# Local attention layers of a gated model on one core: key turn, key scaling, maxima and Gelu moved within their slot

## Chip, cores and metric

The kernel runs on one core of one Trainium2 chip. The metric is the device time of one execution in microseconds.

## The reference, cut to what matters

A residual stream x (4 batches, 256 tokens, 128 features) goes through four gated pairs of a cross attention and a feed-forward block. The change touches one of these eight blocks, `_L0_ffn`, which is itself a stack of six layers of windowed attention with a feed-forward behind each:

```
for i in range(DEPTH):                       # 6
    x = attn_layer(shift_tokens(x), Wqkv[i], q_scale[i], k_scale[i], Wo[i]) + x
    x = ffn_layer(shift_tokens(x), ln_g[i], ln_b[i], W1[i], b1[i], W2[i], b2[i]) + x
```

`attn_layer` has 16 heads of 64. Queries and keys are divided by their norm, scaled and rotated (q * cos + rotate_half(q) * sin). Each token looks at the 32 tokens of its own window and the 32 before, with a mask; then a softmax, the weighted values and the output projection. `ffn_layer` is a layer norm, a projection to 2 x 341, `a * gelu(gate)` and a projection back.

## The kernel before, in words

Everything is float32. The five engines run one program each and meet in semaphores. After a first cross attention (to about 178 us) the local layers run to about 978 us; the other blocks follow in a part called the drain. The change is in the local layers alone.

Their work is cut into 96 units (6 layers x 4 batches x 2 halves of the tokens x 2 halves of the heads, `unit_of`). One unit is 128 tokens x 8 heads x 64. The loops run over 96 slots. In slot s each engine does one step of several units: the projections of unit s, the turns (transposes) of unit s - 2, scores of s - 3, softmax sums of s - 4, weighted values of s - 5, the output of s - 6. The constants TURN, SCORE, SOFT, VALUE, OUT are these lags. Four units make one batch of a layer, and the feed-forward of that batch is spread over later slots by further lags (CENTRE 10 to RENEW 15); `ended(slot, lag)` is true in one slot of four. So slots come in rounds of four. I name a slot by s mod 4: in kind 0 are the gate projections (L663, L672 on TensorE, L1952 on ScalarE), in kind 1 is Gelu (L1966, L1967, a table load before and behind it) with the hidden projections L680 to L689, in kind 2 the centring L256, its variance L266 and the output projection L698 of the feed-forward; kind 3 has none of them on TensorE. The order within a slot is the order of the calls in `pe_local`, `act_local`, `dve_local` and `pool_local`, written by hand. SyncE (`sync_program`) only moves weights and the value windows.

The steps, in the order of a slot, with the line of each:

- TensorE: query projection L722, turn of queries L751, output projection L823, value L742 and key projection L731, turn of the softmax weights L792, scores L781 (64 small matmuls), weighted values L808 (64 small matmuls), turn of keys L759. Turned queries and turned keys share one PSUM bank, so L751 waits for the key copy (`k_kept`) and L759 for the query copy (`q_kept`). L698 and L689 wait for the mask (`masked`) of their slot, since the scores' bank holds their result.
- ScalarE: square of queries L1876, exponential L1921, copies out of PSUM of turned queries L1897, values L1890, square of keys L1883, copy of turned weights L1928, copy of turned keys L1906, copy of the weighted values L1936, then the norms L1912, L1914, L1916 (1/|q| and 1/|k| of the unit, from the sums of squares).
- VectorE: residual L2902, L2903; products with cos and sin for queries and for keys (L2861 to L2863, twice), between them the softmax sum L2891; the mask L2883, maxima L2885; the hidden product L2918 (waits for Gelu); the sums of squares L2870 and L2871.
- GpSimd: division by the softmax sum L4004, sum of the key products L3978, scaling of queries by their norm L3985, sum of the query products L3973, subtraction of the maxima L3998, scaling of keys L3992. In the last slot of a layer it makes the rotary tables of the next (L644).

Of the kernel before, what the change touches and what calls it, by code (L numbers as in the profile page):

```python
# [707 lines left out]
def live(u):  # L708
    return 0 <= u < UNITS
# [126 lines left out]
def pe_local(e, s, m):  # L836
    for slot in range(LOCAL_SLOTS):
        if live(slot):
            pe_query(e, s, m, slot)
        if live(slot - TURN):  # L840
            pe_turn_query(e, s, m, slot - TURN)
        if live(slot - OUT):
            pe_out(e, s, m, slot - OUT)
        if ended(slot, GATES) is not None:
            pe_gates(e, s, m, ended(slot, GATES))
        if live(slot):
            pe_value(e, s, m, slot)
            pe_key(e, s, m, slot)
        if slot == 0:
            e.wait_ge(s["x_done"], B)  # L850
            pe_ln_centre(e, s, m, m.bank[FB], m.x[B - 1])
        if slot == 1:
            pe_ln_var(e, s, m, 2 * B - 1, ln_views(m.ln_local), m.bank[FB])
        if ended(slot, CENTRE) is not None:
            pe_centre(e, s, m, ended(slot, CENTRE))
        if live(slot - VALUE):
            pe_turn_weights(e, s, m, slot - VALUE)
        if live(slot - SCORE):
            pe_scores(e, s, m, slot - SCORE)
        if live(slot - VALUE):  # L860
            pe_weighted(e, s, m, slot - VALUE)
        if ended(slot, VAR) is not None:
            pe_var(e, s, m, ended(slot, VAR))
        if ended(slot, OPEN) is not None:
            pe_hidden(e, s, m, ended(slot, OPEN))
        if ended(slot, LAST) is not None:
            pe_last_hidden(e, s, m, ended(slot, LAST), min(slot - SCORE + 1, UNITS))
        if ended(slot, GATE2) is not None:
            pe_last_gate(e, s, m, ended(slot, GATE2))
        if live(slot - TURN):  # L870
            pe_turn_key(e, s, m, slot - TURN)
        if ended(slot, MERGE) is not None:
            pe_ffn_out(e, s, m, ended(slot, MERGE), min(slot - SCORE + 1, UNITS))

# [1096 lines left out]
def act_local(e, s, m):  # L1971
    for slot in range(LOCAL_SLOTS):
# [18 lines left out]
            act_gates(e, s, m, ended(slot, KEEP))  # L1991
        if ended(slot, SQUARE) is not None:
            act_ln_start(e, s, m, ended(slot, SQUARE))
        if ended(slot, GELU) is not None:
            act_gelu(e, s, m, ended(slot, GELU))
        if live(slot - TURN):
            act_key(e, s, m, slot - TURN)
        if live(slot - VALUE):
            act_out(e, s, m, slot - VALUE)
        if live(slot) and slot >= RAMP:  # L2000
            act_norm(e, s, m, slot)
        if slot == 0:
# [871 lines left out]
def dve_mask(e, s, m, u):  # L2874
# [6 lines left out]
    if u >= ES:  # L2881
        e.wait_ge(s["p_turned"], u - ES + 1)
    e.tensor_tensor(p.rearrange("p (z r k) -> p z r k", z=2, r=UP), scores, band, ALU.add).then_inc(s["masked"], 1)  # L2883
    e.wait_ge(s["masked"], u + 1)
    e.tensor_reduce(m.local_small[u % 4][:, 16:24], split(p, UH), AX.X, ALU.max).then_inc(s["most"], 1)  # L2885


def dve_total(e, s, m, u, link):
# [57 lines left out]
def dve_local(e, s, m, link):  # L2946
    for slot in range(LOCAL_SLOTS):
# [13 lines left out]
            dve_products(e, s, m, slot, 1)  # L2961
        if live(slot - SCORE):
            dve_mask(e, s, m, slot - SCORE)
        if ended(slot, MIX) is not None:
            dve_hidden(e, s, m, ended(slot, MIX))
        if live(slot):
            dve_norm(e, s, m, slot)
        if slot == 2:
            dve_first_z(e, s, m, B - 1, m.bank[FB], ln_views(m.ln_local)[1])

# [1042 lines left out]
def pool_local(e, s, m):  # L4013
    for slot in range(LOCAL_SLOTS):
# [8 lines left out]
            pool_add_query(e, s, m, slot)  # L4023
        if live(slot - 1) and slot <= RAMP:
            pool_norm_key(e, s, m, slot - 1)
        if live(slot - SCORE):
            pool_lower(e, s, m, slot - SCORE)
        if live(slot - 1) and slot > RAMP:
            pool_norm_key(e, s, m, slot - 1)
        if live(slot):  # L4030
            stage = unit_of(slot)[1]
            if slot % (B * LAYER_UNITS) == B * LAYER_UNITS - 1 and stage < DEPTH:
# [570 lines left out]
```

## Time and profile before

| | |
|---|---|
| median of 3 runs | 1283.91 us (1281.17 to 1284.33) |
| span of the profiled execution | 1280.5 us |
| that execution's own time | not given apart from its span |
| TensorE busy | 1215.7 us (95%) |
| VectorE busy | 986.7 us (77%) |
| ScalarE busy | 938.3 us (73%) |
| GpSimd busy | 785.7 us (61%) |
| mean granted TensorE clock | 0.988 of full |

Busy time counts an instruction from start to end; matmuls are pipelined, so a new one starts before the one in front of it ends, and 95% doesn't say that TensorE is at its peak. How far one group of matmuls starts behind another is the better measure of its pace. The span is from the first instruction to the last.

### The profile page before, as it was taken

What the parts mean: (1) busy time and instruction counts of PE and PEld (TensorE: products, weight loads), DVE (VectorE), ACT (ScalarE), POOL (GpSimd) and SP (SyncE); (2) the same over time, 40 slices, a digit from 0 to 9 for tenths busy, and PEclk for the clock granted to TensorE, in tenths of its full rate; (3) what the DMA queues carried; (4) which work ended last, traced back from release to release, by engine and by line L of the source; (5) the groups of instructions that cost most, each with busy time, mean ns of one, the idle gap of its engine ahead of it and who ended that gap; (6) DMA issues with size and microseconds to landing.
All of it is one profiled execution on the core that took longest, in us unless ns stands there. A gap on an engine that the chain in (4) does not pass through costs nothing.

```text
span 1280.5 us, 44796 instructions
## 1 busy us (share of the span) xinstructions
PE 1215.7 (95%) x17900; PEld 871.3 (68%) x17900; DVE 986.7 (77%) x2513; ACT 938.3 (73%) x2310; POOL 785.7 (61%) x805
## 2 busy tenths in 40 slices
PE   7999988999999999999999999999999999999996
PEld 5777745676767667767777677767677877777553
DVE  4666677888888788888888888888888656778677
ACT  6777775677777677777777777777777758788891
POOL 3444447878878787788777877778776102635000
PEclk9999998999999999999999999999999989999989
DMA  5000032222224322342225222422232001202000
GB/s 213 1 2 1 2 116 73 70 61 58 61 62 110 96 60 63 82 127 57 63 59 149 58 63 64 128 79 61 62 86 54 2 15 74 83 32 92 1 1 17
DMA packets 71743, 81.89 MB, mean 64 GB/s; under 512 B 15456, under 2 KB 63584, under 8 KB 71024
## 3 DMA queue, kind: packets, MB, share of 16 engines
q1 hardware_dynamic: 71536, 79.03, 22.4%
q8 instruction: 143, 2.34, 0.8%
q14 instruction: 64, 0.52, 0.1%
HBM read 31.22 MB, written 0.56 MB: 25 GB/s over the span
## 4 chain that ended last, share of the span: by engine, by line
PE 46%; DVE 19%; ACT 18%; issue 11%; POOL 5%; DMA 1%; SPq 0%; DVEq 0%; ACTq 0%; POOLq 0%
PE banks L823 3%; PE banks L808 3%; PE banks L391 2%; DVE arena L2862 2%; DVE arena L2861 2%; DVE small L2870 2%; PE banks L1143 2%; PE banks L1137 2%; PE banks L420 2%; DVE arena L2883 2%; DVE arena L2863 2%; DVE small L2871 2%; PE banks L1165 2%; PE banks L405 2%; PE banks L751 2%
## 5 line engine op out<-in xcount | busy, mean ns | idle before, releaser
L3998 POOL TENSOR_TENSOR arena<-arena,small 128x512 f32<-128x512 f32 x93 | 97.1, 1044 | 136.2 <-DVE small L2885 136.2
L1906 ACT ACTIVATE arena<-banks 128x512 f32<-128x512 f32 x94 | 56.1, 597 | 139.5 <-PE banks L759 139.3
L2861 DVE TENSOR_TENSOR arena<-banks,rotary 128x512 f32<-128x512 f32 x192 | 131.6, 685 | 22.7 <-ACT arena L1876 9.2
L3973 POOL TENSOR_TENSOR arena<-arena 128x512 f32<-128x512 f32 x96 | 122.7, 1278 | 26.3 <-DVE arena L2863 26.2
L808 PE MATMUL banks<-arena 64*64 64x32 f32 x5824 | 107.3, 221 | 15.5 <-issue 8.3
L3978 POOL TENSOR_TENSOR arena<-arena 128x512 f32<-128x512 f32 x95 | 121.4, 1278 | 0.2 <-DVE arena L2863 0.2
L607 POOL TENSOR_TENSOR arena<-arena,small 128x512 f32<-128x512 f32 x64 | 66.6, 1041 | 89.0 <-DVE small L534 89.0
L808 PEld LDWEIGHTS banks<-arena 64*64 64x64 f32 x5824 | 95.8, 135 | 27.0 <-ACT arena L1928 11.4
L3985 POOL TENSOR_TENSOR arena<-arena,small 128x512 f32<-128x512 f32 x95 | 99.5, 1047 | 5.6 <-ACT small L1916 5.6
L722 PE MATMUL banks<-slot,z 128*128 128x512 f32 x192 | 100.1, 603 | 1.3 <-DVE arena L2863 0.9
L3992 POOL TENSOR_TENSOR arena<-arena,small 128x512 f32<-128x512 f32 x95 | 99.2, 1044 | 0.0
L742 PE MATMUL banks<-slot,z 128*128 128x512 f32 x192 | 98.2, 593 | 0.0
L731 PE MATMUL banks<-slot,z 128*128 128x512 f32 x192 | 98.0, 592 | 0.0
L823 PE MATMUL banks<-arena,slot 128*128 128x128 f32 x720 | 97.9, 279 | 0.0
L4004 POOL TENSOR_TENSOR arena<-arena,small 128x512 f32<-128x512 f32 x91 | 95.0, 1044 | 0.0
L751 PEld LDWEIGHTS banks<-constants,arena 128*128 128x128 f32 x376 | 42.0, 142 | 75.4 <-issue 68.1
L461 ACT ACTIVATE arena<-arena,small 128x256 f32<-128x256 f32 x128 | 63.8, 501 | 39.7 <-DVE small L566 39.7
L823 PEld LDWEIGHTS banks<-arena,slot 128*128 128x128 f32 x720 | 88.0, 192 | 0.5
L2902 DVE TENSOR_TENSOR z<-z,banks 64x128 f32<-64x128 f32 x90 | 25.0, 278 | 75.4 <-PE banks L823 75.4
L781 PE MATMUL banks<-arena 64*32 64x64 f32 x5952 | 81.1, 225 | 0.5 <-issue 0.5
L2863 DVE TENSOR_TENSOR arena<-banks,rotary 128x256 f32<-128x256 f32 x192 | 79.6, 415 | 0.0
L2862 DVE TENSOR_TENSOR arena<-banks,rotary 128x256 f32<-128x256 f32 x192 | 79.6, 414 | 0.0
(403 smaller groups left out, 3368.8 us busy)
## 6 DMA issues: line engine op xcount, KB each, us to landing
arena<-arena SPq DMA_DIRECT2D x576, 64.0 KB, 2.1
slot<-in_pack_dram SPq DMA_DIRECT2D x28, 339.5 KB, 3.4
arena<-arena SPq DMA_DIRECT2D x288, 32.0 KB, 1.9
slot<-in_pack_dram SPq DMA_DIRECT2D x2, 2713.5 KB, 9.2
slot<-in_pack_dram SPq DMA_DIRECT2D x1, 2693.5 KB
slot<-in_pack_dram SPq DMA_DIRECT2D x1, 2316.5 KB
arena<-gate_store SPq DMA_DIRECT2D x8, 256.0 KB, 3.9
slot<-in_pack_dram SPq DMA_DIRECT2D x4, 337.0 KB, 3.6
```

The costliest lines, as they stand in the source:

```text
L722: e.matmul(m.bank[QB], m.zs[b][:, t * P:(t + 1) * P], m.W(stage, "Wqkv")[:, half * BANK:(half + 1) * BANK], start=True, stop=True, skip_gr ...
L731: e.matmul(m.bank[KB], m.zs[b][:, t * P:(t + 1) * P], m.W(stage, "Wqkv")[:, at:at + BANK], start=True, stop=True, skip_group_check=True).t ...
L742: e.matmul(m.bank[VB], m.zs[b][:, t * P:(t + 1) * P], m.W(stage, "Wqkv")[:, at:at + BANK], start=True, stop=True, skip_group_check=True).t ...
L808: made = e.matmul(m.bank[PB if x else VB][y * DH:(y + 1) * DH, to:to + WINDOW], v[rows, i, k, :], pT[rows, at:at + WINDOW], start=True, st ...
L823: made = e.matmul(m.bank[S0][:, N:N + P], wo[:, c * D:(c + 1) * D], oT[:, k * P:(k + 1) * P], start=(k == 0), stop=(k == UP - 1), skip_gro ...
L2861: e.tensor_tensor(rot, made, cos, ALU.mult)
L2862: e.tensor_tensor(sinp[:, :, 0:mid], made[:, :, mid:DH], sin[:, :, 0:mid], ALU.mult)
L2863: e.tensor_tensor(sinp[:, :, mid:DH], made[:, :, 0:mid], sin[:, :, mid:DH], ALU.mult).then_inc(s["k_products"] if k else s["q_products"], 1)
L3973: e.tensor_tensor(m.rot_q[u % ROTS], m.rot_q[u % ROTS], m.sin_q[u % 2], ALU.add).then_inc(s["q_added"], 1)
L3978: e.tensor_tensor(m.rot_k[u % ROTS], m.rot_k[u % ROTS], m.sin_k[u % 2], ALU.add).then_inc(s["k_added"], 1)
L3985: e.tensor_tensor(q, q, stretch(m.local_small[u % 4][:, 0:UH], DH), ALU.mult).then_inc(s["q_rotated"], 1)
L3992: e.tensor_tensor(k, k, stretch(m.local_small[u % 4][:, UH:2 * UH], DH), ALU.mult).then_inc(s["k_rotated"], 1)
```

## The change

Four things are moved within a slot, on all four computing engines, and nothing else is touched.

```diff
 def pe_local
         if live(slot - VALUE):
             pe_turn_weights(e, s, m, slot - VALUE)
+        if live(slot - TURN):
+            pe_turn_key(e, s, m, slot - TURN)
         if live(slot - SCORE):
             pe_scores(e, s, m, slot - SCORE)
...
             pe_last_gate(e, s, m, ended(slot, GATE2))
-        if live(slot - TURN):
-            pe_turn_key(e, s, m, slot - TURN)

 def act_local
-        if ended(slot, GELU) is not None:
-            act_gelu(e, s, m, ended(slot, GELU))
         if live(slot - TURN):
             act_key(e, s, m, slot - TURN)
         if live(slot - VALUE):
             act_out(e, s, m, slot - VALUE)
+        if ended(slot, GELU) is not None:
+            act_gelu(e, s, m, ended(slot, GELU))

     e.tensor_tensor(p.rearrange("p (z r k) -> p z r k", z=2, r=UP), scores, band, ALU.add).then_inc(s["masked"], 1)
+
+
+def dve_most(e, s, m, u):
     e.wait_ge(s["masked"], u + 1)
-    e.tensor_reduce(m.local_small[u % 4][:, 16:24], split(p, UH), AX.X, ALU.max).then_inc(s["most"], 1)
+    e.tensor_reduce(m.local_small[u % 4][:, 16:24], split(m.e[u % ES], UH), AX.X, ALU.max).then_inc(s["most"], 1)

 def dve_local
             dve_mask(e, s, m, slot - SCORE)
+        if live(slot):
+            dve_norm(e, s, m, slot)
+        if live(slot - SCORE):
+            dve_most(e, s, m, slot - SCORE)
         if ended(slot, MIX) is not None:
             dve_hidden(e, s, m, ended(slot, MIX))
-        if live(slot):
-            dve_norm(e, s, m, slot)

 def pool_local
+        if live(slot - 1) and slot > RAMP:
+            pool_norm_key(e, s, m, slot - 1)
         if live(slot - SCORE):
             pool_lower(e, s, m, slot - SCORE)
-        if live(slot - 1) and slot > RAMP:
-            pool_norm_key(e, s, m, slot - 1)
```

TensorE in a slot of kind 1, first before and then changed (L792 turns weights, L759 keys, L751 queries; L781 scores, L808 weighted values):

```order
L792 MATMUL banks<-constants,arena 128x128 [waits o_kept,normalised]
L792 MATMUL banks<-constants,arena 128x128 x3
L781 MATMUL banks<-arena 32x64 [waits a2_done,masked,z_ready,y_added,k_kept]
L781 MATMUL banks<-arena 32x64 x31
L808 MATMUL banks<-arena 64x32 [waits v_kept,v64_even,p_kept]
L808 MATMUL banks<-arena 64x32 x31
L680 MATMUL banks<-xn,slot 128x256 [waits gate2_kept]
L681 MATMUL banks<-xn,slot 128x256
L689 MATMUL banks<-xn,slot 85x256 [waits masked]
L759 MATMUL banks<-constants,arena 128x128 [waits q_kept,k_rotated]
L759 MATMUL banks<-constants,arena 128x128 x3
L722 MATMUL banks<-slot,z 128x512 [waits q_products]
```

```order
L792 MATMUL banks<-constants,arena 128x128 [waits o_kept,normalised]
L792 MATMUL banks<-constants,arena 128x128 x3
L759 MATMUL banks<-constants,arena 128x128 [waits q_kept,k_rotated]
L759 MATMUL banks<-constants,arena 128x128 x3
L781 MATMUL banks<-arena 32x64 [waits a2_done,masked,z_ready,y_added,k_kept]
L781 MATMUL banks<-arena 32x64 x31
L808 MATMUL banks<-arena 64x32 [waits v_kept,v64_even,p_kept]
L808 MATMUL banks<-arena 64x32 x31
L680 MATMUL banks<-xn,slot 128x256 [waits gate2_kept]
L681 MATMUL banks<-xn,slot 128x256
L689 MATMUL banks<-xn,slot 85x256 [waits masked]
L722 MATMUL banks<-slot,z 128x512 [waits q_products]
```

The key turn L759 moved from the end of the slot to the place between the turn of the weights and the scores.

ScalarE in the same slot, before and changed (L1928 copies the turned weights, L1906 the turned keys, L1936 the weighted values; L1912 is the first of the norms):

```order
L1928 ACTIVATE arena<-banks 128x512 [waits o_made,p_turned]
L1966 ACT_TABLE_LOAD
L1966 ACTIVATE arena<-arena 128x512 [waits gate2_kept]
L1967 ACTIVATE arena<-arena 85x256
L1968 ACT_TABLE_LOAD
L1906 ACTIVATE arena<-banks 128x4x128 [waits k_turned]
L1936 ACTIVATE arena<-banks 128x512 [waits y_made,o_made]
L1912 ACTIVATE small<-small,eps 128x16 [waits summed]
```

```order
L1928 ACTIVATE arena<-banks 128x512 [waits o_made,p_turned]
L1906 ACTIVATE arena<-banks 128x4x128 [waits k_turned]
L1936 ACTIVATE arena<-banks 128x512 [waits y_made,o_made]
L1966 ACT_TABLE_LOAD
L1966 ACTIVATE arena<-arena 128x512 [waits gate2_kept]
L1967 ACTIVATE arena<-arena 85x256
L1968 ACT_TABLE_LOAD
L1912 ACTIVATE small<-small,eps 128x16 [waits summed]
```

Both copies now stand ahead of Gelu and its table loads, the norms still behind them.

TensorE in a slot of kind 2, changed, from the weighted values to the next query projection (L266 is the variance, L698 the output projection of the feed-forward):

```order
L808 MATMUL banks<-arena 64x32 [waits v_kept,v64_odd,p_kept]
L808 MATMUL banks<-arena 64x32 x31
L266 MATMUL banks<-arena,constants 128x256 [waits ln_squared]
L698 MATMUL banks<-arena,slot 128x256 [waits a2_done,masked]
L698 MATMUL banks<-arena,slot 128x256 x2
L722 MATMUL banks<-slot,z 128x512 [waits q_products]
```

Before, the key turn L759 stood between L266 and L698.

## Rows read from the trace of the kernel before

**Rows 1.** The page, part 4: the chain that ended last, shares by engine.
```profile
PE 46%; DVE 19%; ACT 18%; issue 11%; POOL 5%; DMA 1%; SPq 0%; DVEq 0%; ACTq 0%; POOLq 0%
```

**Rows 2.** Timeline of ScalarE, slots 73, 77, 78: start us, duration us, instruction, [idle before].
```profile
780.67 0.58 ACT L1876 ACTIVATE arena<-banks 128x512 f32<-128x512 f32 x1
...
813.82 0.58 ACT L1876 ACTIVATE arena<-banks 128x512 f32<-128x512 f32 x1
...
815.65 0.59 ACT L1890 ACTIVATE arena<-banks 128x512 f32<-128x512 f32 x1
...
816.61 0.60 ACT L1928 ACTIVATE arena<-banks 128x512 f32<-128x512 f32 x1
817.23 1.28 ACT L1966 ACT_TABLE_LOAD   x1
...
820.77 0.60 ACT L1906 ACTIVATE arena<-banks 128x512 f32<-128x512 f32 x1
...
821.75 0.31 ACT L1912 ACTIVATE small<-small,eps 128x16 f32<-128x16 f32 x1
...
822.55 0.58 ACT L1876 ACTIVATE arena<-banks 128x512 f32<-128x512 f32 x1
...
824.02 0.60 ACT L1890 ACTIVATE arena<-banks 128x512 f32<-128x512 f32 x1
```

**Rows 3.** Line L1966: count, durations ns min/median/max, first and last start us.
```profile
L1966 ACT ACT_TABLE_LOAD  x21: 1283/1283/1283, 273.8 to 954.1; - x21
```

**Rows 4.** Timeline of TensorE, slots 76 to 78.
```profile
811.63 1.02 PE L722 MATMUL banks<-slot,z 128*128 128x512 f32 x2
812.58 0.63 PE L751 MATMUL banks<-constants,arena 128*128 128x128 f32 x4
...
816.22 0.86 PE L781 MATMUL banks<-arena 64*32 64x64 f32 x64
817.26 1.14 PE L808 MATMUL banks<-arena 64*64 64x32 f32 x64 [0.19 <-ACT arena L1928]
...
820.16 1.02 PE L722 MATMUL banks<-slot,z 128*128 128x512 f32 x2
821.52 0.63 PE L751 MATMUL banks<-constants,arena 128*128 128x128 f32 x4 [0.33 <-ACT arena L1906]
...
822.91 1.02 PE L742 MATMUL banks<-slot,z 128*128 128x512 f32 x2
823.77 1.02 PE L731 MATMUL banks<-slot,z 128*128 128x512 f32 x2
...
825.59 0.90 PE L781 MATMUL banks<-arena 64*32 64x64 f32 x64
826.42 1.14 PE L808 MATMUL banks<-arena 64*64 64x32 f32 x64
827.48 0.70 PE L266 MATMUL banks<-arena,constants 128*128 128x256 f32 x2
```

**Rows 5.** Timeline of GpSimd, slot 76.
```profile
811.88 1.05 POOL L3998 TENSOR_TENSOR arena<-arena,small 128x512 f32<-128x512 f32 x1 [0.89 <-DVE small L2885]
```

**Rows 6.** Timeline of VectorE, slot 76: key products, mask, maxima, sums.
```profile
809.13 0.68 DVE L2861 TENSOR_TENSOR arena<-banks,rotary 128x512 f32<-128x512 f32 x1
...
810.40 0.68 DVE L2883 TENSOR_TENSOR arena<-banks,constants 128x512 f32<-128x512 f32 x1
811.11 0.69 DVE L2885 TENSOR_REDUCE small<-arena 128x8 f32<-128x512 f32 x1
811.72 0.68 DVE L2870 TENSOR_REDUCE small<-arena 128x8 f32<-128x512 f32 x1
```

**Rows 7.** Timeline of ScalarE, slots 8 and 9, before any Gelu.
```profile
231.65 0.58 ACT L1876 ACTIVATE arena<-banks 128x512 f32<-128x512 f32 x1
...
239.05 0.58 ACT L1876 ACTIVATE arena<-banks 128x512 f32<-128x512 f32 x1
```

**Rows 8.** Timeline of TensorE, slot 48, behind the rotary tables of a layer.
```profile
572.92 0.66 PE L792 MATMUL banks<-constants,arena 128*128 128x128 f32 x4 [1.10 <-POOL arena L4004]
```

## Prediction, made before the changed kernel was run

> **What bounds the kernel now.** I read the chain of waits first. TensorE holds 46% of it, VectorE 19%, ScalarE 18% [rows 1], so no engine alone sets the time. The timeline of the local layers shows how they share it. I look at one regular round of four slots (slots 73 to 76), from one query square on ScalarE to the one four slots later: 780.67 to 813.82, 33.15 us [rows 2]. There are 21 Gelu slots in this stage (x21 in [rows 3]), one per round.
>
> Now TensorE in and behind the Gelu slot 77 [rows 4]. Starts of matmul groups stand one behind the other at TensorE's own pace nearly everywhere: a 128x512 projection takes 0.86 (822.91 to 823.77) and the scores 0.83 (825.59 to 826.42). It departs from that pace in three kinds of place. The weighted sum L808 waits for the copy of the turned weights, 817.26 - 816.22 = 1.04 in place of 0.83, **0.21**. The turned query L751 behind the projection L722 waits for the key copy that stands behind Gelu on ScalarE, 821.52 - 820.16 = 1.36 in place of 0.86, **0.50**. And in two of the other three slots of a round L751 is **0.09** late (812.58 - 811.63 = 0.95 in place of 0.86), since the key copy of a turn that closes the slot before lands just too late. That is 0.89 us of 33.15, and the rest is work of TensorE that the change only reorders. Gaps in VectorE and GpSimd do not count: the 0.89 us for which GpSimd waits ahead of its subtraction [rows 5] is idle time of an engine that has room.
>
> **The change part by part.** Nothing is added or removed: the same instructions, all four queues reordered, no DMA moved (SyncE's queue is untouched, and the value copy whose windows it loads stays in place).
>
> *Key turn ahead of scores.* The four transposes L759 go from behind the weighted sum to behind L792. The key copy on ScalarE can then be done in the same slot's middle, over a microsecond before L751 asks for it. The two 0.09 and the 0.50 go. The price is that L759 now needs the query copy of its own slot already there. In a usual slot that copy is done well before; behind Gelu it isn't, see below. The weighted sum comes one group of transposes later behind L792, which gives the copy of the weights more room.
>
> *Sums of squares ahead of maxima, key scaling ahead of subtraction.* Now mask 810.40, maxima 811.11, sums from 811.72 [rows 6], then norms, square, and the exponential at 813.82 + 0.48 = 814.30 (the same step as from 815.65 to 816.61, halved) [rows 2]. Reordered, at the pace of 0.61 from one such operation to the next (811.11 to 811.72) [rows 6], the sums start at 811.01 and 811.62 and the maxima at 812.23, ending at 812.92. GpSimd follows 0.08 behind the end of the maxima (811.80 to 811.88) and takes 1.05 [rows 5], so the scores are lowered at 814.05 and the exponential can start there: 0.25 earlier, no more, because the subtraction takes the place of the norms as its last releaser. The key scaling fills GpSimd's wait for nothing; its end hardly moves. The 0.25 covers the 0.21 by which L808 of the Gelu slot is late. That term goes.
>
> *Gelu behind two copies.* This is where a new wait comes in. Gelu with its two table loads blocks ScalarE for 820.77 - 817.23 = 3.54 [rows 2]. Before, it starts at once behind the copy of the weights. Changed, it starts behind the copy of the weighted sums, which waits for L808 of the same slot. The path from L808 of slot 77 to L808 of slot 78 is then: L808 1.14 [rows 4] and about 0.03 to ScalarE; output copy to table load 0.62 (as 816.61 to 817.23); block 3.54; norms 0.80 (821.75 to 822.55); square, exponential and query copy 1.47 (822.55 to 824.02); from there to the weights 0.96 (815.65 to 816.61); weights 0.60, and 0.05 to TensorE [rows 2]. Sum **9.21**. TensorE's own work between the two L808 is 826.42 - 817.26 = 9.16 less the wait of 0.50, 8.66 [rows 4]. So a new wait of 0.55 takes the place of the 0.50: most of it before L759 (query copy), the rest before L808. The interval goes from 9.16 to 9.21, **+0.05**.
>
> Per round: -0.21 - 2 x 0.09 + 0.05 = -0.34, times 21 = **-7.1**.
>
> *The first slots*, before any Gelu, run at 239.05 - 231.65 = 7.40 [rows 7] in the loop square, copies, products, mask, norms, which the reorder shortens by the same 0.25. There are four such slots: **-1**. *The five slots behind the rotary tables*: TensorE waits 1.10 for GpSimd there [rows 8]. The tables now start behind the subtraction, not behind the key scaling; maxima 1.2 later, scaling 1.0 out of the way, so 0.2 later each: **+1**. The bounds of these two together: -3 and +3.
>
> All 21 table loads last 1283 ns [rows 3], and from the start of the first load to the next copy there is 3.54 in all. [...]
>
> The sum is **-7.1** us against the span of this execution, 1280.5 (the page gives the span alone); the median of the three runs is 1283.91, 3.4 above it, and a run differs from another by up to 3. So 1283.9 - 7.1 = 1276.8.
>
> **The rivals.**
>
> *1. The new wait does not come.* If TensorE reaches L808 of the Gelu slot earlier than I think, or the copies behind Gelu go closer together, the 0.55 shrinks. Bound: all waits gone, -0.89 x 21 = -18.7, with the first slots -20: 1264. Against it: the 9.21 is made of rows that hardly vary. Chance 0.12 for anything past -12.
>
> *2. No change.* TensorE is at its pace for over 97% of a round. If reordering costs it a few hundredths per group, or its hiccups eat the slack, little is left: within 3.8 us of now, 1280 to 1288. For it: -0.34 a round is a small difference of large numbers. Chance 0.25.
>
> *3. Slower: two waits in a row behind Gelu.* The output projection of the feed-forward, L698, shares a bank with the scores and waits for the mask of its slot. Now the key turn lies between L266 (827.48) [rows 4] and L698 and covers this. Changed, L698 is wanted behind L808 (1.06, as 826.42 to 827.48) and L266 (at most its 0.70): at most 9.21 + 1.76 = 10.97 from the L808 of slot 77. The mask ends at: square 6.13 (the first five terms of the path above), exponential, query and value copy 1.95, key square 0.60, products 1.27 (809.13 to 810.40), mask 0.68 [rows 2, 6] and 0.1 of handing on, 10.73. So at most 0.24 is spare. VectorE's hidden product L2918 waits for Gelu, now nearly 2 us later, with the residual and both products queued behind it. If it runs late by x, the mask is late by x and TensorE waits once more per round. Break-even is x = 0.24 + 0.34 = 0.58. At x = 1 it is +0.42 x 21 = +9: 1293. Against it: Gelu's results are out ahead of the second table load, at 1.79 + 3.54 - 1.28 = 4.05, and the query products need the square, done at 6.13 + 0.58 = 6.71. So VectorE has 2.7 for the hidden product and three short operations behind it. Chance 0.17.
>
> *4. The Gelu block is longer on the path than in the rows.* [...] The 3.54 of [rows 2], in which two loads and two Gelus follow one another without a gap, speaks against it: chance 0.01. [...]
>
> *5. The reorder at VectorE and GpSimd does nothing by itself*, since TensorE is the bound. This would leave the 0.21, and make it -0.13 x 21 = -3: it is part of rival 2.
>
> **How the numbers follow.** The likeliest case, -4 to -12 around -7.1, has 0.45. Faster by over 0.3% (3.85 us, about what a measurement of this kernel can tell from no change) is 0.45 + 0.12 = 0.57; within it 0.25; slower 0.17 + 0.01 = 0.18. The likeliest case's own range is 1272 to 1280. The range for 8 in 10 leaves out half of rival 1 and half of rival 3: 1267 to 1289.
>
> **What would show it.** Right: L722 to L751 at 0.86 in every slot; L751 never waiting for the key copy; L759 of the slot behind Gelu waiting about 0.5 for the query copy; the interval L808 to L808 across Gelu at 9.2; a regular round near 32.8; ScalarE idle for about 1 us ahead of the output copy in the Gelu slot; GpSimd's key scaling without a wait, its subtraction waiting about 1 us for the maxima. Wrong: L698 waiting for the mask, or L2918 releasing the residual (rival 3); that interval under 9.0 (rival 1); or new gaps at groups of TensorE that have none now.

## Result and the profile after

The changed kernel took **1291.74 us** (median of 4 executions, 1290.78 to 1292.99) against 1283.41 for the kernel before (1281.17 to 1284.33) in the same set of executions: a ratio of **1.0076**, 95% interval 1.0049 to 1.0103. It is slower by 0.8%. The forecast was 1276.8, faster by 0.5%. The profiled execution took 1291.17, its span is 1289.4 against 1280.5, and the granted TensorE clock 0.992 against 0.988, so the clock is no part of it.

Part 1 and part 4 of the page of the changed kernel (the second line answers to [rows 1]):

```profile
PE 1210.1 (94%) x17900; PEld 876.5 (68%) x17900; DVE 980.4 (76%) x2513; ACT 944.1 (73%) x2310; POOL 785.0 (61%) x805
...
PE 50%; POOL 25%; issue 11%; ACT 8%; DVE 5%; DMA 0%; SPq 0%; POOLq 0%; ACTq 0%; DVEq 0%
```

TensorE is busy for 5.6 us less than before, in a span that is 8.9 us longer: it stands still for longer. The chain of waits does not say why. It now runs through GpSimd (25% in place of 5%), and its share of "issue" is 11% as it was. One row of part 5 does say it. First that of the kernel before, then that of the changed one (mean ns of one, then the idle time ahead of the group and its main releaser):

```profile
L808 PE MATMUL banks<-arena 64*64 64x32 f32 x5824 | 107.3, 221 | 15.5 <-issue 8.3 <-ACT arena L1928 6.7
```

```profile
L808 PE MATMUL banks<-arena 64*64 64x32 f32 x5824 | 108.8, 220 | 23.3 <-issue 22.6
```

The wait for the copy of the weights, L1928, is gone, as forecast. In its place "issue", time in which TensorE waited for nothing that the profile shows, grew from 8.3 to 22.6 us. The timeline of TensorE shows where, in slots 74 to 78 (as [rows 4]):

```profile
797.34 0.60 PE L792 MATMUL banks<-constants,arena 128*128 128x128 f32 x4
798.42 0.63 PE L759 MATMUL banks<-constants,arena 128*128 128x128 f32 x4 [0.49 <-ACT arena L1897]
...
807.68 0.86 PE L781 MATMUL banks<-arena 64*32 64x64 f32 x64
808.47 0.78 PE L808 MATMUL banks<-arena 64*64 64x32 f32 x38
810.12 0.65 PE L808 MATMUL banks<-arena 64*64 64x32 f32 x26 [0.87 <-issue]
...
824.55 1.14 PE L808 MATMUL banks<-arena 64*64 64x32 f32 x64
...
827.01 1.02 PE L722 MATMUL banks<-slot,z 128*128 128x512 f32 x2
827.87 0.60 PE L751 MATMUL banks<-constants,arena 128*128 128x128 f32 x4
...
831.35 0.60 PE L792 MATMUL banks<-constants,arena 128*128 128x128 f32 x4
832.44 0.63 PE L759 MATMUL banks<-constants,arena 128*128 128x128 f32 x4 [0.49 <-ACT arena L1897]
833.00 0.86 PE L781 MATMUL banks<-arena 64*32 64x64 f32 x64
833.81 1.13 PE L808 MATMUL banks<-arena 64*64 64x32 f32 x62
836.46 0.24 PE L808 MATMUL banks<-arena 64*64 64x32 f32 x2 [1.52 <-issue]
```

L751 follows L722 at 0.86, L759 comes 0.66 later than its pace of 0.43 behind L792 (832.44 - 831.35 = 1.09), and from one L808 to the next across Gelu it is 833.81 - 824.55 = 9.26. All three are what the forecast drew. But the weighted sums are torn, once behind 38 matmuls and once behind 62. Number TensorE's instructions, a weight load and a matmul as two and each instruction that only waits or signals as one. From the end of the first hole, 810.12, to the end of the second, 836.46, there are 500 matmuls with their loads and 23 others: 1023, which is four times 256 within one. The page's part 3 has a queue that delivers just such pieces:

```profile
q8 instruction: 143, 2.34, 0.8%
```

143 transfers, 2.34 MB: 16 KB each, and TensorE's 36,650 instructions in 143 pieces are 256 each within one. The trace puts one such transfer at 807.34 for 1.32 us and one at 833.93 for 1.07. Both holes end 1.46 us behind the end of their transfer. So I read the holes as **TensorE waiting for its next 256 instructions**. Scores and weighted sums are 128 matmuls and 128 loads in 0.79 + 1.07 us, a whole piece in under 2 us; nothing else in the local layers uses instructions up that fast.

To have one number for a kernel, I took from the trace each step from one matmul to the next, subtracted the usual step (the median) of the same pair of lines, and summed what is left where the matmul starts 1.15 to 1.75 us behind the end of an instruction transfer. I call it the **supply stall**: 15.4 us before, **33.5 after**. 1280.5 - 15.4 = 1265.1 and 1289.4 - 33.5 = 1255.9: without the stalls the change gains 9.2. A wait for something else that ends in that time by chance is counted too. What stands where a new piece begins, at instruction number 193 or 194 modulo 256 (counted from 0), is 12.1 us before and **30.0 after**: 17.9 more, against 18.1 by the wider count.

Not all "issue" is supply. The first query projection of a layer waits for that layer's weights, which SyncE loads, and the page has this under "issue" too. Slot 64 of the changed kernel, where the last two loads (L4398) are issued at 702.22 and 702.85 and the last has landed at 708.44:

```profile
704.80 1.14 PE L808 MATMUL banks<-arena 64*64 64x32 f32 x64
708.53 1.35 PE L722 MATMUL banks<-slot,z 128*128 128x512 f32 x2 [2.59 <-issue]
```

Before, the last load of that layer had landed at 701.75, and L722 started at 702.1 without a wait. In the changed trace two layers begin with such a wait, 1.1 and 2.6 us (the row of L722 on the page has 3.9 <-issue); in the trace before one does, with 0.4. This belongs to the waits, not to the stalls. With one trace of each kernel, how much of it is the change's doing isn't shown.

### The profile page after: what moved, and what is told of

Same layout as the page of the kernel before. It is cut to its first block, busy times and chain, and to the rows that moved or that the text cites. A ratio compares the mean times of both kernels' runs of the same rounds, so it can differ in the third digit from the quotient of the medians.

```text
span 1289.4 us, 44796 instructions
## 1 busy us (share of the span) xinstructions
PE 1210.1 (94%) x17900; PEld 876.5 (68%) x17900; DVE 980.4 (76%) x2513; ACT 944.1 (73%) x2310; POOL 785.0 (61%) x805
## 3 DMA queue, kind: packets, MB, share of 16 engines
q8 instruction: 143, 2.34, 0.8%
## 4 chain that ended last, share of the span: by engine, by line
PE 50%; POOL 25%; issue 11%; ACT 8%; DVE 5%; DMA 0%; SPq 0%; POOLq 0%; ACTq 0%; DVEq 0%
POOL arena L3978 5%; POOL arena L3983 5%; POOL arena L4003 4%; PE banks L808 4%; POOL arena L4009 4%; POOL arena L3997 4%; PE banks L781 3%; PE banks L722 2%; PE banks L391 2%; POOL arena L3990 2%; PE banks L823 2%; PE banks L742 2%; PE banks L731 2%; ACT arena L2186 2%; PE banks L1143 2%
## 5 line engine op out<-in xcount | busy, mean ns | idle before, releaser
L808 PE MATMUL banks<-arena 64*64 64x32 f32 x5824 | 108.8, 220 | 23.3 <-issue 22.6
L1936 ACT ACTIVATE arena<-banks 128x512 f32<-128x512 f32 x91 | 54.4, 597 | 103.2 <-PE banks L808 103.2
L808 PEld LDWEIGHTS banks<-arena 64*64 64x64 f32 x5824 | 96.5, 134 | 34.4 <-issue 25.0
L722 PE MATMUL banks<-slot,z 128*128 128x512 f32 x192 | 103.1, 619 | 4.8 <-issue 3.9
L742 PE MATMUL banks<-slot,z 128*128 128x512 f32 x192 | 98.2, 593 | 0.0
L731 PE MATMUL banks<-slot,z 128*128 128x512 f32 x192 | 98.0, 592 | 0.0
L823 PE MATMUL banks<-arena,slot 128*128 128x128 f32 x720 | 96.6, 278 | 0.0
L823 PEld LDWEIGHTS banks<-arena,slot 128*128 128x128 f32 x720 | 89.0, 194 | 0.1
L751 PEld LDWEIGHTS banks<-constants,arena 128*128 128x128 f32 x376 | 47.5, 143 | 54.4 <-issue 49.0
L781 PE MATMUL banks<-arena 64*32 64x64 f32 x5952 | 80.6, 224 | 0.0
L792 PEld LDWEIGHTS banks<-constants,arena 128*128 128x128 f32 x364 | 45.0, 141 | 46.3 <-issue 24.0
```

Source lines behind the costliest of these rows:

```text
L722: e.matmul(m.bank[QB], m.zs[b][:, t * P:(t + 1) * P], m.W(stage, "Wqkv")[:, half * BANK:(half + 1) * BANK], start=True, stop=True, skip_gr ...
L731: e.matmul(m.bank[KB], m.zs[b][:, t * P:(t + 1) * P], m.W(stage, "Wqkv")[:, at:at + BANK], start=True, stop=True, skip_group_check=True).t ...
L742: e.matmul(m.bank[VB], m.zs[b][:, t * P:(t + 1) * P], m.W(stage, "Wqkv")[:, at:at + BANK], start=True, stop=True, skip_group_check=True).t ...
L808: made = e.matmul(m.bank[PB if x else VB][y * DH:(y + 1) * DH, to:to + WINDOW], v[rows, i, k, :], pT[rows, at:at + WINDOW], start=True, st ...
L823: made = e.matmul(m.bank[S0][:, N:N + P], wo[:, c * D:(c + 1) * D], oT[:, k * P:(k + 1) * P], start=(k == 0), stop=(k == UP - 1), skip_gro ...
```

## Experiments

In the expectations, W is the theory of waits alone (the prediction's, with the loss somewhere in semaphores), F that of the instruction supply. All kernels with their medians, ratios against the kernel before in the same set of executions, supply stalls, the part of them at number 193 or 194, and the "issue" idle time of L808. The kernel before had a median of 1283.4 beside the changed kernel, 1283.5 beside k1 to k4, 1280.3 beside k5, k6, k7 and k9, 1283.7 beside k8 and k11 to k13, and 1285.4 beside k14 and k15. So between sets the ratios are the better comparison: k9 is 3.7 us below k4, but only 0.15% by the ratios.

| kernel | us | ratio (95%) | stalls, us | at 193/194 | L808 issue, us |
|---|---|---|---|---|---|
| before | 1283.4 | | 15.4 | 12.1 | 8.3 |
| changed | 1291.7 | 1.0076 (1.0049 to 1.0103) | 33.5 | 30.0 | 22.6 |
| k1, keys' turn alone | 1292.9 | 1.0084 (1.0053 to 1.0115) | 36.6 | 31.7 | 24.6 |
| k2, VectorE and GpSimd alone | 1277.2 | 0.9951 (0.9931 to 0.9971) | 22.9 | 18.9 | 13.9 |
| k3, Gelu alone | 1400.3 | 1.0915 (1.0872 to 1.0959) | 17.0 | 12.5 | 10.0 |
| k4, changed without Gelu's part | 1277.9 | 0.9969 (0.9945 to 0.9992) | 30.2 | 23.7 | 17.0 |
| k5, changed, numbers shifted by 64 | 1299.5 (one) | | 35.5 | 32.3 | 23.5 |
| k6, changed, split everywhere | 1312.6 | 1.0237 (1.0198 to 1.0275) | 9.0 | 4.5 | 2.6 |
| k7, before, split everywhere | 1328.0 | 1.0373 (1.0343 to 1.0403) | 2.8 | 0.0 | 0.0 |
| k9, k4 split everywhere | 1274.2 | 0.9954 (0.9937 to 0.9972) | 3.8 | 1.2 | 0.5 |
| k11, k4 split in 25 slots of the window | 1264.0 | 0.9840 (0.9815 to 0.9864) | 12.5 | 7.0 | 3.6 |
| k12, k4 split in 25 other slots | 1273.7 | 0.9915 (0.9890 to 0.9941) | 27.7 | 22.3 | 16.7 |
| k13, changed, split in the window | 1288.8 | 1.0032 (1.0008 to 1.0056) | 15.1 | 12.9 | 8.2 |
| k8, changed, keys between | 1280.0 | 0.9968 (0.9948 to 0.9989) | 13.1 | 10.7 | 7.2 |
| k14, k4, keys between | 1273.7 | 0.9918 (0.9893 to 0.9942) | 16.9 | 12.8 | 8.6 |
| k15, k14 split in the window | 1267.3 | 0.9868 (0.9851 to 0.9884) | 6.8 | 3.8 | 2.3 |

The difference between the two stall columns, 2 to 7 us, is waits elsewhere that end in the same time by chance, for the most part at L751, L823 and in the drain. In all 16 traces together the weighted sums of the local layers hold 197 holes of over 0.25 us between two starts. Every one ends at instruction number 193 or 194 modulo 256.

### The parts, one by one

k1 and k2 are the kernel before with one part of the diff shown ahead (TensorE's; VectorE's and GpSimd's), k3 that with ScalarE's, and k4 the changed kernel without ScalarE's:

```diff
# k1, TensorE alone
+        if live(slot - TURN):
+            pe_turn_key(e, s, m, slot - TURN)
         if live(slot - SCORE):
             pe_scores(e, s, m, slot - SCORE)
...
# k4, on the changed kernel
+        if ended(slot, GELU) is not None:
+            act_gelu(e, s, m, ended(slot, GELU))
         if live(slot - TURN):
             act_key(e, s, m, slot - TURN)
         if live(slot - VALUE):
             act_out(e, s, m, slot - VALUE)
-        if ended(slot, GELU) is not None:
-            act_gelu(e, s, m, ended(slot, GELU))
```

> The kernel before with the key turn moved on TensorE alone. Two theories on the 9 us lost. W (waits): what counts are the semaphore waits; then the two 0.09 of a round go, the 0.50 behind Gelu stays: -4, 1279. F (fetch): TensorE's instructions are brought in by 16 KB pieces of 256 instructions, and the 256 instructions of scores and weighted values run in 1.9 us, less than a piece takes to come; with the key turn ahead of them the piece that holds them is run through faster, and the gaps inside L808 grow from 12 us in all to about 20: 1283 to 1288.

> The kernel before with the new order on VectorE and GpSimd alone. W: the wait of 0.21 ahead of L808 in the Gelu slot goes, 1 us in the first slots: -5, 1278. F: the same, less what the gaps in L808 take back when the wait ahead of it is gone, 1 to 3 us: 1279 to 1282.

> The kernel before with Gelu behind the two copies alone. The key turn still closes the slot, so the key copy comes at 3.2 us behind the start of L808 and Gelu 4.2 us later than before; the path from L808 to the next L808 is 11.7 in place of 9.16: +2.5 x 21 = +53, about 1335, by both theories; by F the gaps in L808 shrink to a few us, since the fetch runs on while TensorE waits.

> The changed kernel with Gelu back ahead of the two copies. W: 0.21 and the two 0.09 go, 0.50 stays: -0.39 x 21 = -8, 1275. F: the gaps in L808 are nearly those of the changed kernel, 20 to 25 us in place of 12: 1283 to 1288.

k1 is as slow as the whole change, and it has the stalls (36.6): F has the kind, not the size, and W is far off. k2 is faster (-6.3 us against the 1283.5 beside it), though its stalls rise by 7.5: the earlier exponential takes away waits of TensorE, and what that saves outweighs the stalls. k4 came near W's number and not into F's range, although its stalls are 30.2: W's gains are as real as F's stalls, and neither alone gives a time. The parts do not add up: the keys' turn costs 9.3 us alone (k1), but 0.6 on top of k2's part (k4 against k2), where it brings 7.3 of stalls and saves about as much in waits. k4 also shows that Gelu's part, which should have been worth nothing much, costs 13.9 on top of the other two, and only 3.3 of that are stalls. From k4's trace to the changed one TensorE's start at L759 is late by 12 us more in the local layers, at L751 by only 8 less, and at L722, where a layer's weights are waited for, by 4 more.

k3 was expected at about 1335 and came at 1400. Its cause is that of the prediction's third rival, a late hidden product, but at other places and worse than drawn. The keys' turn stands at the end of the slot here, so both copies and then Gelu wait for it. Timeline of TensorE in k3, then the same stretch cut in two, with busy time and granted clock:

```profile
639.80 0.67 PE L256 MATMUL banks<-z,constants 128*128 128x256 f32 x2 [0.43 <-DVE arena L2918]
...
642.10 0.85 PE L781 MATMUL banks<-arena 64*32 64x64 f32 x64 [1.20 <-DVE arena L2926]
644.78 1.93 PE L808 MATMUL banks<-arena 64*64 64x32 f32 x64 [1.83 <-ACT arena L1928]
```

```profile
640.00:645.00 5.00, 1.98 (x78) 1.51 (x81) 4.48 (x12) 4.06 (x10) 2.32 (x2) 0.93 0.00 1
645.00:650.00 5.00, 5.00 (x74) 4.38 (x71) 3.20 (x7) 1.25 (x3) 2.87 (x3) 0.50 0.28 68
```

The columns of the second fence are the stretch, its length, busy time (and count) of matmuls, weight loads, VectorE, ScalarE and GpSimd, the granted clock, the DMA share and GB/s. The hidden product L2918 releases TensorE late, then the scores and the weighted sums wait again, 3.5 us of idle in one slot. Behind it the granted clock is 0.50, with TensorE busy for 5.00 of 5.00 us, where it had been busy for 1.98 of the 5.00 before. TensorE's idle time in the whole trace is 131.2 us against 64.8 (span less busy time), and its busy time 1270.3 against 1215.7 for the same 17,900 matmuls, with 138 us at a granted clock of 0.50 against 33 (a mean of 0.951 against 0.988). So about half the price of ScalarE's part alone is waits, and the other half, 54.6 us, is clock.

### The numbers shifted

k5 puts 128 waits that are already fulfilled, 64 instructions (44,860 in its trace against 44,796), into slot 5 of the changed kernel. Every later instruction has a number higher by 64, and nothing else changes.

```diff
+        if slot == 5:
+            for _ in range(128):
+                e.wait_ge(s["x_done"], B)
         if live(slot - VALUE):
             pe_turn_weights(e, s, m, slot - VALUE)
```

> The changed kernel, with 128 waits on a long reached semaphore added to TensorE's queue in slot 5, two to an instruction, so 64 instructions: everything behind them stands 64 further in its 256-instruction piece, and nothing else changes. Counted from the start of TensorE's queue, the scores of a slot begin at some place modulo 256, and the gaps inside L808 stood in the slots where this is about 190 to 250 (slots 9, 13, 17, 42, 46, 50, 53, 57, 60, 78, 82, 86, 89, 93 and others). Fetch: they leave these slots and come in those that stood at 126 to 190 (8, 12, 16, 23, 27, 34, 41, 45, 49, 52, 56, 63, 70, 74, 81, 85, 88, 92). Another theory, that they come from what Gelu or the value windows do in a slot, leaves them where they are. Time within 8 of the changed kernel's.

The time itself says little (a single execution; the pad and what it delays stand in the first slots). The places say much. From slot 20 on the changed kernel has 16 slots with a stall of 0.7 us or more, and in 15 of them the scores begin at a number from 186 to 254 modulo 256. With the shift there are again 16, 14 of them with scores from 186 to 254, and only 31, 49 and 78 are the same slots. Slot 77 had no hole; it has one now, at number 194, outside the burst:

```profile
838.51 0.59 PE L681 MATMUL banks<-xn,slot 128*128 128x256 f32 x2
840.70 0.59 PE L689 MATMUL banks<-xn,slot 128*85 128x256 f32 x2 [1.59 <-issue]
```

The holes follow the number, not the work. That speaks against waits and against memory traffic, which belong to slots and not to numbers.

### The burst split everywhere

The next query's projection L722, two wide matmuls of 0.86 us, goes between scores and weighted sums in every slot: k6 from the changed kernel, k7 from the one before, k9 from k4.

```diff
-        if live(slot):
+        if slot == 0:
             pe_query(e, s, m, slot)
...
             pe_scores(e, s, m, slot - SCORE)
+        if live(slot + 1) and slot + 1 < LOCAL_SLOTS:
+            pe_query(e, s, m, slot + 1)
         if live(slot - VALUE):
             pe_weighted(e, s, m, slot - VALUE)
```

> The changed kernel with the next slot's query projection L722 (4 instructions, 0.86 us) taken in between scores and weighted values. Fetch: a piece that held almost only the two bursts now lasts 0.86 longer, so each gap is 0.86 shorter and half go: gaps 29 to about 9, time -15 to -20, 1272 to 1277. Waits alone: the same work in another order, no gain, and up to 0.36 a slot more for L823, which waits for the output copy: 1292 to 1300.

> The kernel before with the same move of L722. Fetch: gaps 12 to 2 or less, -8 to -10 less what L823 waits more: 1274 to 1280. Waits alone: 1284 to 1290.

> The changed kernel without the Gelu move, and with L722 between scores and weighted values. Fetch: gaps 26 to about 8, -14 to -18 less what L823 waits more, 0.36 in one slot of four, 9 in all at most: 1262 to 1272. Waits alone: 1278 to 1286.

The stalls go in all three (33.5 to 9.0, 15.4 to 2.8, 30.2 to 3.8), as F says, and the times of k6 and k7 miss both theories, while k9 is 2 us above F's range (5 above it, if the 3 us are counted by which the kernel before was faster in that set). The page of k7 and the timeline of k6 show what F had left out:

```profile
L722 PE MATMUL banks<-slot,z 128*128 128x512 f32 x192 | 108.5, 647 | 8.3 <-issue 7.4
...
L751 PE MATMUL banks<-constants,arena 128*128 128x128 f32 x376 | 58.5, 278 | 58.3 <-ACT arena L1908 54.5
```

```profile
593.07 0.86 PE L781 MATMUL banks<-arena 64*32 64x64 f32 x64
593.86 1.13 PE L722 MATMUL banks<-slot,z 128*128 128x512 f32 x2
594.92 1.14 PE L808 MATMUL banks<-arena 64*64 64x32 f32 x64
595.98 0.70 PE L680 MATMUL banks<-xn,slot 128*128 128x256 f32 x2
...
600.86 0.60 PE L792 MATMUL banks<-constants,arena 128*128 128x128 f32 x4
602.80 0.63 PE L759 MATMUL banks<-constants,arena 128*128 128x128 f32 x4 [1.34 <-ACT arena L1899]
```

First, L722 had been the cover between the keys' turn and L751. In k7 the two stand side by side, and L751 waits for the keys' copy in every slot, 54.5 us. Second, in k6 L722 no longer stands between L808 of the Gelu slot and L759 of the next, so the wait there grows by just its 0.86: 602.80 - 600.86 - 0.43 = 1.51 in place of 0.65, some 20 times, 17 us. Third, L808 follows L722 at 1.06 (594.92 - 593.86) where other wide matmuls are followed at 0.86: 0.19 in each of 90 slots, 17 us. Fourth, a new layer's first L722 now comes earlier and waits for the weights four times, up to 3.7 us, 10.5 in all in k6 against 3.9 in the changed kernel. For k6: -24 + 17 + 17 and 7 for the layers is +17. L823, which waits for the output copy as the expectation had said, is 8 later in all, and the waits behind the rotary tables are 4 shorter: +21, as measured.

### The burst split where the numbers say

If F is right, most of this price buys nothing: only the slots need the split whose burst meets the end of a piece. k11 splits 25 slots of k4, those whose scores begin at 186 to 254 modulo 256; k12 splits 25 others with as many of each kind of slot; k13 is the changed kernel with k11's slots.

```diff
+AHEAD = (5, 9, 13, 17, 20, 21, 24, 28, 31, 35, 42, 46, 49, 53, 57, 60, 64, 67, 71, 75, 78, 82, 86, 89, 93)
...
-        if live(slot):
+        if live(slot) and slot - 1 not in AHEAD:
             pe_query(e, s, m, slot)
...
             pe_scores(e, s, m, slot - SCORE)
+        if slot in AHEAD and live(slot + 1):
+            pe_query(e, s, m, slot + 1)
```

> The change without its Gelu part, with the next query's projection (L722, two matmuls of 512 columns) placed between scores and weighted sums in 25 slots alone: those whose scores begin with TensorE's instruction number 186 to 254, modulo 256. Instruction supply (F): every gap inside the weighted sums ended at an instruction number of 193 or 194 modulo 256, and there are 26.5 us of such gaps in the kernel without the Gelu part and 1.5 us when all slots are split. Splitting these 25 takes away nearly all of them (gaps under 5 us) at 25 x 0.19 us for the weight load that follows L722: 1277.9 - 22 + 5 = 1261, between 1257 and 1266. Waits (W: the gaps come of the order of the work, wherever the numbers lie): a quarter of what splitting all slots brought (3.7 us), so 1276 to 1278.

> The same as the run before it, with the projection moved in 25 other slots, as many of each kind, whose scores begin with an instruction number of 25 to 165 modulo 256. F: no gap is taken away, and the 25 moves cost 0.19 us each: 1277.9 + 5 = 1283, between 1279 and 1286, with gaps of 24 to 29 us. W: 1276 to 1278, the same as the run before it.

> The whole change, with the projection moved in the 25 slots of the window. F: gaps fall from 29.1 us to under 6, for 5 us of weight loads; some 10 of the 25 slots hold the Gelus, where moving L722 away from ahead of the keys' turn lets the wait behind the query's copy grow from 0.65 to 1.5 us (as it did when all slots were split): +8. 1291.7 - 23 + 5 + 8 = 1282, between 1277 and 1287. W: within 2 us of 1291.7 or above it.

> The kernel of the run k11_split_in_window once more, against a wider set of runs: F: a ratio of 0.984, between 0.981 and 0.987 (1264 us). If the split's gain was a chance of the first set of executions: 0.990 or more.

k11 lands in F's range, 1264.0, and again at 1265.2 (0.9854, 0.9829 to 0.9878) in a second set. Slot 60, whose scores begin at number 204, in k4, k12 and k11:

```profile
670.38 0.86 PE L781 MATMUL banks<-arena 64*32 64x64 f32 x64
671.17 1.11 PE L808 MATMUL banks<-arena 64*64 64x32 f32 x58
674.18 0.31 PE L808 MATMUL banks<-arena 64*64 64x32 f32 x6 [1.89 <-issue]
```

```profile
667.62 0.86 PE L781 MATMUL banks<-arena 64*32 64x64 f32 x64
668.40 1.11 PE L808 MATMUL banks<-arena 64*64 64x32 f32 x58
671.43 0.31 PE L808 MATMUL banks<-arena 64*64 64x32 f32 x6 [1.91 <-issue]
```

```profile
660.79 0.86 PE L781 MATMUL banks<-arena 64*32 64x64 f32 x64
661.57 1.12 PE L722 MATMUL banks<-slot,z 128*128 128x512 f32 x2
662.63 1.02 PE L808 MATMUL banks<-arena 64*64 64x32 f32 x56
664.28 0.32 PE L808 MATMUL banks<-arena 64*64 64x32 f32 x8 [0.64 <-issue]
```

204 + 128 for the scores + 116 for 58 weighted sums is 448 = 256 + 192: the hole stands where the sum says. With 1.06 us of other work in the burst it shrinks by 1.25, to 0.64; it isn't gone. I had expected under 5 us of stalls in the local layers, and there are 10.1 (12.5 in all). But only 7.0 of them stand at 193 or 194, where k4 has 23.7; 3.6 are waits of L751, which the move of L722 has not touched.

k12 keeps its stalls, 27.7, as F says, and is 9.7 slower than k11 in the same set. But it is faster than expected, 1273.7 in place of 1279 to 1286. Its waits at L751 are 8.7 us against 15.3 in k4, which is about the size of the miss; why a moved projection saves them there and not in k11 (13.0) I leave open. W, which wanted the two kernels equal, is out.

k13 came out 2 us above its range. The wait at L759 grew as expected, from 13.1 to 21.0 us; the stalls fell by 18 and not by 23, as in k11; and the wait for a layer's weights at L722, which the expectation had left out, is 7.8 us in place of 3.9.

### Keys between scores and weighted sums

The other place for the turn of the keys: behind the scores. k8 has it in the changed kernel, k14 in k4, and k15 is k14 with k11's split.

```diff
-        if live(slot - TURN):
-            pe_turn_key(e, s, m, slot - TURN)
         if live(slot - SCORE):
             pe_scores(e, s, m, slot - SCORE)
+        if live(slot - TURN):
+            pe_turn_key(e, s, m, slot - TURN)
         if live(slot - VALUE):
             pe_weighted(e, s, m, slot - VALUE)
```

> The whole change, but the turn of the keys (L759, four matmuls) between the scores and the weighted sums. F: the burst of 256 small instructions is broken by 0.43 us of work and the piece of the instruction stream has that much more time: gaps fall by about 0.4 us in each of 20 slots (29 to about 21); the wait behind the query's copy in 21 Gelu slots (0.65 us each) is covered by the scores: -13; a load of small weights behind L759 costs up to 0.10 us in 92 slots: +9. 1291.7 - 8 - 13 + 9 = 1280, between 1275 and 1286. If only waits matter (W): 1291.7 - 13 = 1279, with gaps unchanged; the gaps in the trace tell the two apart, not the time.

> The change without its Gelu part, with the keys' turn (L759) between scores and weighted sums. F: gaps about 10 us, as in the run with the keys between and the Gelus behind (9.6), against 26.5 us without it; the load of small weights behind L759 costs 0.15 us in 91 slots less 0.10 us at the scores: +5; the Gelu slots' wait stays at L751 (0.5 us in some 15 slots). 1277.9 - 16 + 5 = 1267, between 1262 and 1272. W (order and waits alone): 1278 to 1283.

> The same, and the projection L722 also between the keys' turn and the weighted sums in the same 25 slots of the window. F: gaps under 3 us; up to 0.19 us more in 25 slots (less where L759 has paid for it already): 1267 - 8 + 3 = 1262, between 1257 and 1267. W: 1266 to 1268, no gain on the run before it.

k8's time is right and its reasons are half wrong. The stalls fell by 20, not 8, and the wait behind Gelu was not covered: it moved to L808, 0.55 in each Gelu slot. k14 is 2 us above its range: stalls fell by 13, where 16 was expected, and the order costs 14, not 5. From the turn of the weights to the weighted sums it is 0.53 + 0.79 + 0.58 = 1.90 in k14 and 0.44 + 0.53 + 0.79 = 1.76 in k4, about 0.15 in each of 91 slots; I had subtracted 0.10 that the scores pay in either order. These two alone would leave k14 where k4 is; it is 4 faster, and its trace shows waits at L751 and L823 that are some 4 us shorter. k15 has few stalls, 6.8, and is still no faster than k11 in the same set (1267.3 against 1265.2, intervals that overlap). The cures add up in stalls but not in time. k11 and k15 are the fastest kernels, and the runs don't tell them apart; k11 is 1.5 to 1.6% faster than the kernel before and 2.2 to 2.3% faster than the changed one.

## Why the prediction was wrong

*Key turn ahead of scores.* Both 0.09 and the 0.50 at L751 went. The usual steps from one query square on ScalarE to the next are 7.49, 7.69, 7.34 and 10.34, a round of 32.86 where 33.15 - 0.34 = 32.81 was forecast. **The step that failed is "the rest is work of TensorE that the change only reorders", and with it the cost of nothing for the order itself.** In the kernel before, the weighted sums had 12 holes with 11 us; in the changed one 21 with 27. In the whole kernel the stalls grew from 15.4 to 33.5 us, which the sum had at nothing. The order now puts eight instructions of 54 ns each (four transposes in 0.43 us) right ahead of the burst, and the 0.21 at L808 in which a transfer could catch up is gone. That these two are what makes the holes more and longer is my reading. The runs show that the keys' turn alone brings 21 us of stalls (k1), that taking away most of the wait for L1928 at L808 (6.7 to 2.2 us) brings 7.5 (k2), and that 1.06 us of wide work inside the burst takes 1.25 off one hole (k11).

*Sums ahead of maxima, key scaling ahead of subtraction.* Right: L808 waits for L1928 only once, 0.5 us, GpSimd's subtraction waits for the maxima, its key scaling waits for nothing. The part is worth -6.3 us alone (k2), more than the 0.21 a round in the forecast, in spite of 7.5 of new stalls.

*Gelu behind two copies.* Where no hole comes in between, the path was right: 9.26 where 9.21 was forecast, ScalarE idle for 1.06 ahead of the output copy, L759 late by 0.65, and the block again 3.54 from the first load to the norms (826.37 to 829.91):

```profile
825.75 0.60 ACT L1936 ACTIVATE arena<-banks 128x512 f32<-128x512 f32 x1 [1.06 <-PE banks L808]
826.37 1.28 ACT L1966 ACT_TABLE_LOAD   x1
827.66 0.63 ACT L1966 ACTIVATE arena<-arena 128x512 f32<-128x512 f32 x1
...
829.91 0.31 ACT L1912 ACTIVATE small<-small,eps 128x16 f32<-128x16 f32 x1
```

But k4 against the changed kernel puts this part at +13.9, where I had +1: this is the second term that failed. What the sum left out is a link: a stall in a Gelu slot now delays the end of L808, with it the output copy, with it Gelu, and the wait at L759 comes on top. With Gelu ahead of the copies the stall and the Gelu block run side by side. Slot 53 shows it, in the changed kernel and then in k4, up to the next L808 (which starts at 626.77 and 621.44):

```profile
618.26 0.42 PE L808 MATMUL banks<-arena 64*64 64x32 f32 x11 [0.80 <-issue]
...
625.40 0.63 PE L759 MATMUL banks<-constants,arena 128*128 128x128 f32 x4 [0.46 <-ACT arena L1897]
```

```profile
613.60 0.42 PE L808 MATMUL banks<-arena 64*64 64x32 f32 x11 [1.07 <-issue]
...
616.21 0.60 PE L751 MATMUL banks<-constants,arena 128*128 128x128 f32 x4
```

From L808 to L808 it is 10.32 in the changed kernel, 9.26 and the whole hole; in k4, with a longer hole, only 9.92 (9.25 without one), since the hole takes the place of L751's wait. Over the 21 Gelu slots the changed kernel takes 7.5 us longer than k4, 1.9 of it longer holes. The larger part, 12.5, is lost in the slots behind them: there the changed kernel has 9.6 us of holes in its weighted sums and k4 has 0.6, though TensorE has the same instructions at the same numbers in both. The other slots give 3 back. So the number says where a hole can stand, and not whether one does; why it stands there in the one kernel and not in the other is not shown.

*First slots and tables.* -1 was forecast for the first slots; they gained more, about 4 us by slot 12. Behind the tables TensorE is 1.4 late in place of 1.3, as small as forecast.

*The rivals.* Rival 4 (chance 0.01), a Gelu block longer on the path than in the rows, did not come: all 21 blocks of the changed kernel take 3.54 to 3.55, as the 3.54 of [rows 2]. Rival 3 (L698 waiting for the mask) did not come in the changed kernel: VectorE waits for Gelu at the hidden product there, 27.5 us in 19 slots, and L698 doesn't wait. In k3 the hidden product is so late that TensorE waits for it, but at L256, L781 and L808, not at L698, and at many times the rival's price. Rival 2 had named "hiccups" without a mechanism; they were the case. The rows for it were there: the page's 8.3 us of issue ahead of L808 in the kernel before, which no semaphore explains.

The account: waits and order -9.2 (forecast -7.1), instruction supply +18.1 (forecast nothing), together +8.9 in the span. That the first is near its forecast is luck: stalls aside, the first two parts together gained 20 us where 8 or 9 had been drawn (k4: -5.6, with 14.8 more of stalls), and Gelu's part cost 11 where 1 had been drawn.

## What to carry over

Idle time that the page calls "issue" in the middle of a group of equal instructions costs time like other waits: k11 has 17.7 us less in stalls than k4 and is 13.9 us faster. Number the engine's instructions, and see if the holes end at one number modulo 256 (here 193 or 194). Where a burst of small instructions uses up a piece faster than the next one comes (here 256 in 1.9 us, while the two holes of the changed kernel end 2.8 and 2.5 us behind the start of their transfer), a wait or slow work ahead of it or inside it can cost nothing, and a change that takes it out can gain nothing there, as in slot 53 of k4, where the hole takes the place of L751's wait (9.92 against 10.32 from L808 to L808). Break the burst with wide work, only where the numbers call for it (k11, 1264.0 us, against k12, 1273.7), and first ask what that work was covering.

## What the hardware showed that I had not expected

- TensorE, as I read it, runs out of instructions. The hole ends 1.2 to 1.7 us behind the end of a 16 KB transfer that itself takes 0.9 to 1.6, always at number 193 or 194 modulo 256. What passes in these 1.2 to 1.7 us isn't shown, nor what starts the transfer: in the local layers of the changed kernel it starts between 7 and 250 instructions ahead of the end of a piece, and no fixed number fits.
- A burst of 64-row loads behind a 128x512 matmul starts 1.06 behind it where another wide matmul starts 0.86 behind: 0.19 each time.
- In k3 the granted clock was 0.50 in a stretch behind one in which TensorE was busy for 1.98 of 5.00 us, and the lower level cost nearly as much as the waits did (54.6 of 117 us).
